# FFN activations split in SBUF and transposed by DMA instead of on TensorE, with the first rounds reordered

## The reference

```python
def ffn(x):                                   # DIM 128, HIDDEN 384, weights int / 127
    gate = einsum('bsd,hd->bsh', x, wg)
    up   = einsum('bsd,hd->bsh', x, wu)
    return einsum('bsh,dh->bsd', silu(gate) * up, wd)

def attn(x):                                  # 4 heads, 2 kv heads, head dim 32
    h = rmsnorm(x, norm_w)
    q, k, v = h @ Wq, h @ Wk, h @ Wv          # q, k l2-normalised per head
    a = softmax(causal(q @ k.T * exp(log_temperature)))
    return x + gate * ((a @ v) @ Wo)

x = x + 0.5 * ffn(layernorm(x))
x = x + attn(layernorm(x))
x = x + 0.5 * ffn(layernorm(x))
```

## Time and profile before

| | us |
|---|---|
| median of 3 runs | 493.02 |
| the 3 runs | 497.06, 491.48, 493.02 |
| the profiled execution | 495.74 |
| its span | 493.9 |

### The profile page before, as it was taken

How to read it: one execution, slowest core, us unless ns; L and a number is a source line. 1 busy time by engine, 2 the same in 40 slices (tenths; PEclk the granted TensorE clock), 3 DMA queues, 4 the chain that set the end, 5 groups by cost and what they waited for, 6 DMA issues and landing times.

```text
span 493.9 us, 11179 instructions
## 1 busy us (share of the span) xinstructions
PE 433.7 (88%) x3862; PEld 232.3 (47%) x3862; DVE 369.4 (75%) x876; ACT 388.0 (79%) x554; POOL 244.2 (49%) x357
## 2 busy tenths in 40 slices
PE   0779999972797999999999999999999987999994
PEld 0447676651242543534434525435344344767673
DVE  4988899968749577968869869777646448888762
ACT  3589988663486798897897887988968977999971
POOL 3566779543643544454273445441223206777742
PEclk9999999997788999999999999999999998999997
DMA  6610000023311605209216033072050000211212
GB/s 170 186 49 3 0 1 0 0 44 79 72 21 42 132 2 127 46 1 140 32 30 140 0 90 80 1 129 45 1 129 1 0 1 2 66 51 55 63 43 70
DMA packets 85451, 26.50 MB, mean 54 GB/s; under 512 B 67872, under 2 KB 85408, under 8 KB 85408
## 3 DMA queue, kind: packets, MB, share of 16 engines
q1 hardware_dynamic: 84400, 25.76, 23.3%
q10 hardware_dynamic: 1008, 0.20, 0.2%
HBM read 4.98 MB, written 4.19 MB: 19 GB/s over the span
## 4 chain that ended last, share of the span: by engine, by line
PE 58%; DVE 16%; issue 11%; POOL 6%; ACT 5%; DMA 1%; POOLq 1%; DVEq 1%; SPq 0%; ACTq 0%
PE ps L403 12%; PE ps L585 11%; PE ps L566 9%; PE ps L590 9%; PE ps L451 5%; PE ps L445 4%; DVE H L276 2%; PE ps L474 2%; DVE X L869 2%; PE ps L396 2%; PE ps L612 2%; PE ps L570 2%; ACT PT L687 2%; ACT SG L362 2%; POOL OL L240 1%
## 5 line engine op out<-in xcount | busy, mean ns | idle before, releaser
L687 ACT ACTIVATE PT<-ps,k_exp 128x1024 f32<-128x1024 f32 (+1 forms) x192 | 162.7, 901 | 25.4 <-PE ps L570 20.1
L566 PE MATMUL ps<-QKT 128*128 128x512 f16 (+3 forms) x384 | 90.1, 337 | 21.5 <-ACT PT L687 12.4
L403 PE MATMUL ps<-XT,WT 128*128 128x512 f16 x384 | 95.9, 389 | 9.2 <-DVE H L276 6.2
L327 POOL TENSOR_TENSOR HL<-H,HH 128x1024 f16<-128x1024 f32 x32 | 68.5, 2139 | 45.1 <-ACT HH L366 45.1
L585 PE MATMUL ps<-PT,V 128*32 128x512 f32 (+3 forms) x768 | 83.6, 508 | 1.0 <-ACT PVS L721 1.0
L590 PE MATMUL ps<-PT,ones 128*32 128x512 f32 (+3 forms) x768 | 79.9, 487 | 0.0
L240 POOL TENSOR_TENSOR OL<-ON,OH 128x512 f16<-128x512 f32 x16 | 19.4, 1212 | 94.2 <-ACT OH L236 94.2
L276 DVE SCALAR_TENSOR_TENSOR H<-SG,k_isilu,ps 128x1536 f32<-128x1536 f32 x32 | 57.9, 1808 | 10.2 <-ACT SG L362 7.3
L566 PEld LDWEIGHTS ps<-QKT 128*128 128x128 f16 x384 | 28.5, 99 | 78.4 <-ACT PT L687 58.8
L403 PEld LDWEIGHTS ps<-XT,WT 128*128 128x128 f16 x384 | 37.0, 100 | 46.0 <-issue 8.4
L230 DVE RECIPROCAL RD<-PVS 128x512 f32<-128x512 f32 x16 | 53.4, 3340 | 3.7 <-ACT PVS L721 3.5
(11 more groups left out here) (120 smaller groups left out, 675.0 us busy)
## 6 DMA issues: line engine op xcount, KB each, us to landing
X<-in_L_attn_x SPq DMA_DIRECT2D x16, 256.0 KB, 2.9
result<-X SPq DMA_DIRECT2D x16, 256.0 KB, 2.3
AXT<-AS SPq DMA_TRANSPOSE x16, 3.1
QKT<-ST SPq DMA_TRANSPOSE x16, 4.6
w_int<-in_L_ffn_w_gate SPq DMA_DIRECT2D x1, 192.0 KB, 3.5
w_int<-in_L_ffn_w_up SPq DMA_DIRECT2D x1, 192.0 KB, 4.4
w_int<-in_L_ffn_w_down SPq DMA_DIRECT2D x1, 192.0 KB, 5.0
qkvo<-in_L_attn_Wq ACTq DMA_DIRECT2D x1, 64.0 KB, 2.2
```

The lines of the kernel that those rows point to most:

```text
L327: e.tensor_tensor(HL[k % 2][:, :, :], H[k % 2][:, NW:, :], HH[k % 2][:, :, :], ALU.subtract).then_inc(s_hl, 1)
L403: i = e.matmul(out[:, j, :], WT[:, wp, w * NJ + j, :], XT[k % 2][:, xp, :], start=a == 0, stop=a == len(passes) - 1)
L566: i_ = e.matmul(o, QKT[k % 2][:, i // TPC, NH + hp, i % TPC * P:(i % TPC + 1) * P], QKT[k % 2][:, qc, 2 * hp + h, CH - n:CH], start=True, ...
L687: e.activation(PT[g % 2][:, 2 * hp:2 * hp + 2, 0:n], SCORES[hp][:, :, 0:n], ACT.Exp, scale=k_exp[:, 0:1]).then_inc(a_exp, 1)
```

## The change

- **Transposing.** `x_t` is gone from PE. `x_hi` and `x_lo` now work on `XN` in SBUF and write the float16 tile `XS` (which lies in the memory of `w_int`). SP's `turn_ffn` transposes `XS` into `XT` by one DMA per chunk. It waits for `x_lo(c)` and for `up(c-2)`. `x_lo` has moved from DVE to POOL, one tensor_tensor per chunk. `gate_` waits for the DMA.
- **Layer norm factors.** `NM` and variance + eps move from POOL to DVE, as `scaled`: two tensor_scalar of 128x4 elements behind `aggregate`. POOL keeps the power and `NB`. There are eight buffers of `RS`, `NM` and `NB` in place of two.
- **Leads.** Per round `i`: DVE does hidden(i), stats(i+6), residual(i-1), aggregate(i+6), scaled(i+6); POOL does x_lo(i+3), rstd(i+5), h_lo(i); ACT does silu(i), x_hi(i+3), normalise(i+4), h_hi(i); PE does gate(i+1), down(i-1), up(i+1).
- **Loads.** `X` is loaded in six pieces (1, 1, 2, 4, 4 and 4 chunks), all issued at once and ahead of the first `turn_ffn`.
- **Start of the first FFN.** The transposes of the low parts of the weights on PE come behind gate(0), DVE's copies of them behind its moments of chunk 2 and ahead of those of chunks 3 to 5. The scaling of attention's weights moves from before hidden(0) to behind rounds 0, 1 and 2. `is_hot` on DVE (a register load) moves to the start of attention.
- **Attention's first steps.** DVE normalises the four tiles of a chunk in one round (10 and 12), where it did two tiles in each of four rounds.
- **Start of the second FFN.** Six chunks have their moments and three their split before the FFN starts. POOL does `x_hi` for chunks 0 to 2. The last output projection goes to the bank `XP` in round 1 (it was `DN` in round 0), and the last reciprocal is in two halves with hidden(0) between them.
- **SP** issues the transposes of the second FFN and the stores in one sequence, a store four chunks behind.

```diff
         XT = [sb(f"XT{i}", [P, 2, CH], f16) for i in range(2)]
+        w_words = w_int.rearrange("p j n -> p (j n)")
+        XS = [w_words[:, i * CH:(i + 1) * CH].bitcast(f16).rearrange("p (s t n) -> p s t n", s=2, t=TPC)
+              for i in range(2)]
...
+        loads = [(0, 1), (1, 2), (2, 4), (4, 8), (8, 12), (12, 16)]
...
+        def last_reciprocal(e, half):
+            m = 2 * B - 1
+            cols = slice(half * CH // 2, (half + 1) * CH // 2)
+            e.wait_ge(a_pvc, 2 * m + 2)
+            e.wait_ge(a_ol, m)
+            i = e.reciprocal(RD[:, cols], PVS[:, 1, cols])
+            if half:
+                i.then_inc(a_rd, 1)
+                e.wait_ge(a_rd, m + 1)
+                e.tensor_tensor(ON[:, :], PVS[:, 0, :], RD[:, :], ALU.mult).then_inc(a_on, 1)
...
+            def scaled(k, c):
+                g = c + NC * ph
+                e.wait_ge(s_stat, 3 * g + 2)
+                if ph and k < NE + 2:
+                    e.wait_ge(s_xn, NC)
+                elif k >= NE + 2:
+                    e.wait_ge(s_xn, g - 1)
+                e.tensor_scalar(NM[slot(k)][:, :], MV[k % 2][:, :, 0], -1.0, None, ALU.mult)
+                e.tensor_scalar(RS[slot(k)][:, :], MV[k % 2][:, :, 1], LN_EPS, None, ALU.add)\
+                    .then_inc(s_stat, 1)
...
-            pipeline(e, [(0, hidden), (2, x_lo), (1, last_o_norm), (5, stats), (5, sums_there),
-                         (0, last_wo_out), (-1, residual), (5, aggregate)],
+            pipeline(e, [(0, hidden), (6, stats), (6, sums_there), (0, last_wo_out), (-1, residual),
+                         (6, aggregate), (6, scaled)],
                      early, after, end)
...
+            def x_hi(k, c):
+                g = c + NC * ph
+                e.wait_ge(s_xn, g + 1)
+                e.wait_ge(d_f[k % 2], (g - k % 2) * 8)
+                e.tensor_copy(XS[k % 2][:, 0, :, :], XN[k % 2][:, :, :]).then_inc(s_xh, 1)
+
+            def x_lo(k, c):
+                e.wait_ge(s_xh, c + NC * ph + 1)
+                e.tensor_tensor(XS[k % 2][:, 1, :, :], XN[k % 2][:, :, :], XS[k % 2][:, 0, :, :],
+                                ALU.subtract).then_inc(s_xl, 1)
...
-            pipeline(e, [(4, rstd), (0, h_lo)], sum(early, []), after, end)
+            pipeline(e, [(0, last_o_lo), (3, x_lo), (5, rstd), (0, h_lo)], early, after, end)
...
-            pipeline(e, [(0, silu), (2, x_hi), (0, last_o_hi), (3, normalise), (0, first_out),
+            pipeline(e, [(0, silu), (0, last_o_hi), (3, x_hi), (4, normalise), (0, first_out),
                          (0, h_hi)],
...
-            pipeline(e, [(1, gate_), (-1, down), (1, up), (0, last_wo), (3, x_t)], early,
-                     after)
+            pipeline(e, [(1, gate_), (-1, down), (0, last_wo), (1, up)], early, after, 2)
...
-            HEAD = {5: 0, 6: 1, 7: 2, 9: 3}
+            HEAD = {5: 0, 6: 1, 8: 2, 10: 3}
...
+        def turn_ffn(e, ph, c):
+            g = c + NC * ph
+            e.wait_ge(s_xl, g + 1)
+            if g >= 2:
+                e.wait_ge(s_up, g - 1)
+            e.dma_start(XT[c % 2].rearrange("p s (t n) -> p (s t) n", n=P),
+                        XS[c % 2].rearrange("p s t n -> p (s t) n"), transpose=True)\
+                .then_inc(d_f[c % 2], 16)
...
+            ffn_dve(e, 0, None, {-4: low_parts, 0: weights_scaled, 1: weights_low, 2: weights_factors,
+                                 6: first_rows("stats", 0),
+                                 7: first_rows("stats", 1),
+                                 10: first_rows("normalise", 0),
+                                 12: first_rows("normalise", 1),
+                                 NC - 1: lambda: att_dve(e, False, "units")}, 5)
...
+            def finish():
+                last_reciprocal(e, 0)
+                ffn_dve(e, 1, [("hidden", 0)])
+                last_reciprocal(e, 1)
+                ffn_dve(e, 1)
```

More of the change, by code:

```diff
@@ L240, in o_lo, with slot, loaded, ffn_dve @@
             e.tensor_tensor(OL[:, :], ON[:, :], OH[:, :], ALU.subtract).then_inc(a_ol, 1)
-        def ffn_dve(e, ph, when=None, after={}, end=0):
+        def slot(k):
+            return 2 + k if k < NE else k % 2
+        def loaded(e, c):
+            for i, (lo, hi) in enumerate(loads):
+                if lo <= c < hi:
+                    e.wait_ge(s_xin[i], 16)
+        def ffn_dve(e, ph, only=None, after={}, end=0):
             def stats(k, c):
-                if ph == 0:
-                    e.wait_ge(s_xin[k % 2], (c - k % 2) * 8 + 16)
+                if ph == 0 and isinstance(c, int):
+                    loaded(e, c)
                 g = c + NC * ph
                 if k >= 1 or ph:
-                    e.wait_ge(s_stat, 2 * g)
+                    e.wait_ge(s_stat, 3 * g - 1)
                 for t in range(TPC):
@@ L263, in aggregate, with moments @@
                 i.then_inc(s_stat, 1)
[L265 to L268, removed]
+            def scaled(k, c):
[8 more added lines that the diff above has]
+                    .then_inc(s_stat, 1)
+            def moments(k, c):
+                stats(k, c)
+                sums_there(k, c)
+                aggregate(k, c)
+                scaled(k, c)
             def hidden(k, c):
@@ new lines, in ffn_dve @@
+            if only is not None:
+                ops = dict(stats=stats, sums_there=sums_there, aggregate=aggregate, scaled=scaled,
+                           moments=moments, hidden=hidden)
+                for name, c in only:
+                    ops[name](c, c)
+                return
+            early = [(op, c) for c in range(NE if ph else 2)
+                     for op in (stats, sums_there, aggregate, scaled)]
+            if ph:
+                early += [(hidden, 0)]
+            pipeline(e, [(0, hidden), (6, stats), (6, sums_there), (0, last_wo_out), (-1, residual),
+                         (6, aggregate), (6, scaled)],
@@ L833, in step @@
                     x_lo(m0 + 3, 1)
+                if not nxt:
+                    ffn_pool(e, 1, [("x_hi", 2), ("x_lo", 2), ("rstd", 4), ("rstd", 5)])
             drive(e, step, B, 1, 3)
-            o_lo(e, B * 2 - 1)
         def att_dve(e, shift, first=None):
@@ L971, in step @@
                 if not nxt:
-                    ffn_dve(e, 1, 0)
+                    ffn_dve(e, 1, [("moments", c) for c in range(4)])
                 if later:
@@ L996, in step @@
                 if not nxt:
-                    ffn_dve(e, 1, 1)
+                    ffn_dve(e, 1, [("moments", c) for c in range(4, NE)])
                 wo_out(k, b, ("wo", 0), b * 2)
@@ L1073, in _ @@
                     .then_inc(s_out, 16)
-            e.wait_ge(s_out, NC * 16)
+            def finish():
+                for c in range(NC + 4):
+                    if c < NC:
+                        turn_ffn(e, 1, c)
+                    if c >= 4:
+                        store(c - 4)
+                e.wait_ge(s_out, NC * 16)
+            by_heat(e, turn, hot, finish)
         @block.gpsimd
@@ L1186, in _ @@
             i.then_inc(s_wprep, 1)
-            ffn_dve(e, 0, 2)
+            ffn_dve(e, 0, [("sums_there", 1), ("aggregate", 1), ("scaled", 1)])
+            k_values()
             e.wait_ge(s_wprep, 3)
```

269 lines of the change are left out of this document (122 added, 147 removed).

## The result

The changed kernel takes 504.28 us (median of 4 runs, 503.66 to 504.62) against 494.38 (491.48 to 497.06, 4 runs) for the kernel before: ratio 1.020, 95% interval 1.0135 to 1.0265. It is slower by 9.9 us. The profiled execution took 503.66 us with a span of 501.8, against 495.74 and 493.9: 7.9 more. The forecast was 518, inside its range of 491 to 527, with the right sign and more than double the size.

The account below looks back on a forecast made before the run. PE set the 4.87 us round; the change was to make it 6.2 through two DVE waits on POOL. First FFN 16.4, attention 0.8 and second FFN 8.2 gave 25.4 on 495.74, 521.1; the median 2.7 lower, 518.4, range 491 to 527.

Parts of the forecast that it names:

- The mechanism: Steady FFN rounds: NM on DVE waits for POOL's HL to end at 5.10 us, closing the loop hidden, HH, HL, scaled.
- `RS` waits for its end, 5.05 + 1.15 = 6.2: Steady FFN rounds: RS also waits for x_lo on POOL, making the round 6.2 us; two waits per round had chance 0.54.
- Rival 1: Only one wait per round, if x_lo is ready later: 5.35 us a round, about 501 us; chance 0.13.
- The start: Up to the first FFN's hidden(0): first transpose held behind queued loads, landing at 21.6, hidden(0) at 30.7; +4.1 us.
- Weights' pieces, stats, `rstds`: First FFN, rounds 0 to 9: attention's weight scaling +2.0, its stats behind RS +1.7, rstds letting RS through -1.0 us.
- Rounds 10 to 14: End of first FFN, without scaled: three rounds of 4.45 and two with four AN tiles at 5.5; -3.5 us.
- Attention: Register load moves from the head to attention's start on DVE: +0.8 us, between 0 and 0.9; the rest as before.
- the head of the second FFN: Table load at about 401.0, then half a reciprocal ahead of hidden(0), bringing it to 405.0 us.
- Second FFN's rounds: Eight rounds of 6.2 and five of 4.45 us after hidden(2) at 418.4; hidden(15) at 490.3 against 482.11, +8.2.
- No wait: Rival: four-element strided operations don't wait for POOL, rounds of 4.6 us, about 491.5 us; chance 0.29.
- late transposes: Rival: DMA transposes landing over 6 us bind the round, or PE's clock falls; over 527 us; chance 0.04 together.

Follow-up runs that it names:

- e1_psum: Changed kernel with the moments that NM and RS read in a free PSUM bank instead of SBUF (second FFN: from chunk 7 on); 497.64 us.
- e3_before_dve: Kernel before, with only -mean and var+eps moved to VectorE tensor_scalar behind bn_aggr; 504.77 us, ratio 1.020.
- e6_start: Changed kernel with NM and RS right behind hidden, x loads issued later, low weights turned before gate(0), attention's weights scaled before hidden(0); 487.83 us.

## Why the prediction was right and wrong

- **The mechanism** (a four-column tensor_scalar from SBUF to SBUF waits for a running HL, and the loop closes): right. NM ended 0.02 us after HL; e1_psum took the wait away and with it the loop; e3_before_dve brought it into the kernel before.
- **"`RS` waits for its end, 5.05 + 1.15 = 6.2"**: the step that failed, a size and not the mechanism. RS took 0.15 us and the round 5.11. The row that I leaned on was AN's. A reading that fits, but that no run tested, is that its 128 columns keep DVE busy beyond HL's end, so that POOL's next operation gets in ahead of the second AN, and that NM's four columns don't. I gave 0.54 to a case that turned on hundredths of a microsecond. The rule that I had cited from the Trainium skill fits NM, which waited; on RS, whose start is on record 0.02 us ahead of x_lo's, the forecast went beyond it. Rival 1 had this case at 5.35 and 501 us, with 0.13; its condition, x_lo ready only after HL's end, was not met (x_hi ended at 55.11, before HL) and RS still came first. Some twenty rounds at 1.09 us too much are 21.8 us. Set to 5.11, the sum of 25.4 becomes 3.6, below the 7.9 measured, so other terms were too low. (The addends of the start's 30.7 make 30.6.)
- **The start** (+4.1): +5.2. The landing was forecast at 21.6, for an issue at 14, and came at 23.2, for an issue at 16.66: 6.5 us, against 3.1 at the median, and at most 4.7 in e6_start, where fewer loads were queued. So the transpose was held, but by 1.8 to 3.4 us and not by 4.3. Missed: ACT's small loads landed up to 2.6 us later and w_down 1.3. Three chunks' moments ahead of hidden(0) were as forecast.
- **Weights' pieces, stats, `rstds`** (+2.0, +1.7, -1.0): rounds 0 and 1 took 12.8 us against 9.2, +3.6 with the waits. The cast of QKVO (35.53, 2.17 us) ended 0.22 us behind HL's end and its subtraction (42.86, 1.52) 0.43 us behind x_lo's; in the kernel before, where no such operation of POOL ran beside them, they took 0.36 and 0.56.
- **Rounds 10 to 14** (-3.5): +0.4. I gave AN's rounds 5.5 us. In the profile after, the second group took 3.41 us and its round 7.46, behind HL and then AS, which is just what rows 4 showed; I had priced it at half.
- **Attention** (+0.8, and -3.6 at the head of the second FFN): together -6.8 instead of -2.8. About 3.1 go with the granted clock, which the sum held constant: so much shorter is the distance in e3_before_dve, which differs from the kernel before only in NM and RS. That leaves some 3.7, near the forecast.
- **Second FFN's rounds**: 5.11 instead of 6.2 for nine rounds, and a first round of 7.56 against 6.36 before (forecast 7.2): +2.8 instead of +11.8.

No wait (0.29) and late transposes (0.04) are refuted for this kernel: NM waited up to 1.43 us, and a landing took 3.1 us at the median, 6.5 at most, at the start. The price of the no-wait rival was too low as well: e1_psum, in which NM and RS hardly wait, took 497.64 us and not 491.5.

## What to carry to other kernels

Before you move even a four-element operation to VectorE, ask what GpSimd does at that point of the order and whether the operation has all of its operands in SBUF; behind a long GpSimd subtraction it doesn't cost its own 0.16 us but everything up to that subtraction's end, and if the subtraction hangs on VectorE's next big product, the round becomes that loop. Mend it by place (behind the product) or by operand (a source in PSUM), each some 7 us of 504 here. Queue bulk loads behind what the first stage waits for, and treat a wait that is decided within 0.1 us as two cases with their own prices, not as one. Where versions differ by 1 or 2 us, compare them by stretch, with the granted clock beside each, before you credit an edit.
